# Second mixing stage: the squares of the last sixteen channels are added up by TensorE

## What is computed

```python
h = layer_norm(x, ni_w, ni_b)
h = (h @ pi_w.T + pi_b) * jax.nn.sigmoid(h @ gi_w.T + gi_b)
h = h * mask[..., None]
a1, b1, a2, b2 = jnp.split(h.astype(jnp.float32), 4, axis=-1)
x1 = jnp.einsum('bikd,bjkd->bijd', a1, b1)
x2 = jnp.einsum('bkid,bkjd->bijd', a2, b2)
h = jnp.concatenate([x1, x2], axis=-1).astype(h.dtype)
h = layer_norm(h, no_w, no_b)
return (h @ po_w.T + po_b) * jax.nn.sigmoid(h @ go_w.T + go_b)
```

## Time and profile before

| | |
|---|---|
| three timed runs | 1553.26, 1548.57, 1548.98 us, median 1548.98 |
| profiled execution | 1551.37 us, of which the span is 1549.5 |
| busy over the span | PE 89%, DVE 78%, ACT 63%, POOL 39% |
| granted TensorE clock, mean | 0.958 of 2.4 GHz |

### The profile page before, as it was taken

The page is one execution under the profiler, slowest core; times in us unless marked ns, Lnnn a source line. Parts: engine busy times, 40 slices in busy tenths (PEclk is TensorE's granted clock), DMA queues, the critical chain, the costliest instruction groups (busy, mean ns, idle before and its releaser), DMA issues. The chain is left out here.

```text
span 1549.5 us, 26748 instructions
## 1 busy us (share of the span) xinstructions
PE 1380.6 (89%) x9158; PEld 765.4 (49%) x9163; DVE 1213.9 (78%) x2073; ACT 977.9 (63%) x1576; POOL 607.1 (39%) x389
## 2 busy tenths in 40 slices
PE   6778897888797997999989999898999979997897
PEld 5427432222585442344469998222244447773443
DVE  6644787799699886999957776998799968998664
ACT  5675588834344787878846666356877856662555
POOL 6400298320000893299400000596359800003665
PEclk9898999999899998999989999899999999998999
DMA  9368210057785220499988886795189899996998
GB/s 356 130 190 313 96 55 2 1 164 205 264 296 206 83 94 1 164 336 341 345 304 299 306 299 226 272 373 215 46 331 344 341 325 391 418 395 230 392 389 313
DMA packets 152693, 381.62 MB, mean 246 GB/s; under 512 B 15728, under 2 KB 15984, under 8 KB 152432
## 3 DMA queue, kind: packets, MB, share of 16 engines
q1 hardware_dynamic: 140176, 356.64, 63.4%
q10 hardware_dynamic: 12384, 23.28, 4.1%
HBM read 191.11 MB, written 188.74 MB: 245 GB/s over the span
## 5 line engine op out<-in xcount | busy, mean ns | idle before, releaser
L1201 PE MATMUL banks<-work 128*128 128x256 f32 x1408 | 337.0, 388 | 16.1 <-DVE work L1274 6.7
L1201 PEld LDWEIGHTS banks<-work 128*128 128x128 f32 x1408 | 263.1, 196 | 63.3 <-issue 17.4
L1561 POOL TENSOR_TENSOR xT<-xT,work 128x512 f32<-128x512 f32 x192 | 241.3, 1273 | 58.9 <-DVE work L1610 56.0
L740 PE MATMUL banks<-work,w 64*64 64x512 f32 x2048 | 256.9, 595 | 3.3 <-DVE work L938 3.1
L978 DVE SCALAR_TENSOR_TENSOR work<-banks,bias,work 128x512 f32<-128x512 f32 x256 | 188.1, 748 | 29.7 <-PE banks L740 25.6
L856 ACT ACTIVATE work<-banks,bias 128x512 f32<-128x512 f32 x256 | 171.9, 686 | 42.1 <-PE banks L740 41.5
L1233 ACT COPY work<-banks 128x512 f32<-128x512 f32 x176 | 103.3, 587 | 144.9 <-PE banks L1201 141.0
L1372 POOL MEMSET work<- 32x2048 bf16 x4 | 7.2, 1800 | 469.2 <-issue 370.2
L1300 DVE TENSOR_TENSOR work<-work 128x512 f32<-128x512 f32 x176 | 121.2, 689 | 58.2 <-ACT work L1233 57.1
L1610 DVE SCALAR_TENSOR_TENSOR work<-banks,bias,work 128x512 f32<-128x512 f32 x192 | 142.0, 748 | 30.9 <-ACT work L1535 15.1
L909 POOL TENSOR_TENSOR work<-work,cols 128x512 f32<-128x512 f32 x2 | 163.9, 81970 | 0.3
(11 more groups left out here) (172 smaller groups left out, 2278.2 us busy)
## 6 DMA issues: line engine op xcount, KB each, us to landing
hidden_rows<-work SPq DMA_DIRECT2D x128, 512.0 KB, 4.1
work<-hidden_rows SPq DMA_DIRECT2D x120, 512.0 KB, 6.8
products<-work SPq DMA_DIRECT2D x88, 512.0 KB, 3.8
work<-products SPq DMA_DIRECT2D x88, 512.0 KB, 4.7
work<-gate_rows SPq DMA_DIRECT2D x64, 512.0 KB, 5.4
work<-hidden SPq DMA_DIRECT2D x40, 512.0 KB, 6.1
work<-in_x SPq DMA_DIRECT2D x32, 512.0 KB, 5.1
gate_rows<-work SPq DMA_DIRECT2D x32, 512.0 KB, 3.1
```

The lines of the kernel that those rows point to most:

```text
L740: mm = pe.matmul(out[side, :], w(name)[rows, side], h[rows, t % H, :], start=True, stop=True)
L1201: mm = pe.matmul(ZB[c % 2][:, r * N:r * N + N], a[:, kk, rows_of(r, c)], x[:, kk, :], start=(kk == 0), stop=(kk == 1))
L1561: pool.tensor_tensor(columns(t), columns(t), term[:, t % RING, :], ALU.add).then_inc(x_sb, 1)
```

## The change

For channels 16 to 31 of the second mixing stage, VectorE no longer adds the squares to `s2`. TensorE does, with products of the identity and the buffer of squares that accumulate in bank 7. The first of them (for channel 16) is preceded by one that brings in `s2` as it stands after 16 channels. `square_sums(c - 2)` follows `product(c - 1)` in the loop. The last one stands behind the clock-keeping products, which go to bank 6 now. ScalarE's square waits for the identity product of two channels back where it waited for VectorE. The variance step reads bank 7 in place of `s2`.

```diff
+    squares_on_tensor = masked_load
...
+            def square_sums(c):
+                if c < 0 or not squares_on_tensor(c):
+                    return
+                if c == turned:
+                    pe.wait_ge(s2_sb, turned)
+                    pe.matmul(bank[7][:, :], core.ident[:, :], s2, start=True, stop=False).then_inc(s2_mm, 1)
+                pe.wait_ge(sq_sb, c + 1)
+                pe.matmul(bank[7][:, :], core.ident[:, :], sq[:, c % 2, :], start=False,
+                          stop=c == channels - 1).then_inc(s2_mm, 1)
...
                 turn(c)
                 if c:
                     product(c - 1)
+                square_sums(c - 2)
             product(channels - 1)
-            core.keep_clock(pe, 4, bank[7])
+            square_sums(channels - 2)
+            core.keep_clock(pe, 4, bank[6])
+            square_sums(channels - 1)
...
-                at_least(act, s2_sb, c - 1)
+                if c >= 2 and squares_on_tensor(c - 2):
+                    act.wait_ge(s2_mm, c - turned)
+                else:
+                    at_least(act, s2_sb, c - 1)
...
                 dve.tensor_tensor(s1, s1, zs[:, c % (2 * OUT), :], ALU.add).then_inc(s1_sb, 1)
+                if squares_on_tensor(c):
+                    return
                 dve.wait_ge(sq_sb, c + 1)
...
-        finish(core, 1, 2, None, mask, sums, out)
+        finish(core, 1, 2, None, mask, [sums[0], core.bank[7]], out)
```

More of the change, by code:

```diff
@@ L1098, in mix @@
         (mask_in, mask_mm, mask_sb, masked_a, masked_b, turn_mm, ta_sb, tb_sb, z_mm, z_sb, sq_sb, s1_sb, s2_sb, begun,
-         shifted) = core.sems(f"mix{layer}", "mask_in mask_mm mask_sb masked_a masked_b turn_mm ta_sb tb_sb z_mm z_sb "
-                              "sq_sb s1_sb s2_sb begun shifted")
+         shifted, s2_mm) = core.sems(f"mix{layer}", "mask_in mask_mm mask_sb masked_a masked_b turn_mm ta_sb tb_sb z_mm "
+                                     "z_sb sq_sb s1_sb s2_sb begun shifted s2_mm")
         single = core.sems(f"mix{layer}", " ".join(f"single{c}" for c in range(SINGLES)))
@@ L1409, in on_tensor @@
     def on_tensor(self, pe):
-        self.core.keep_clock(pe, 4, self.core.bank[7])
+        self.core.keep_clock(pe, 4, self.core.bank[6])
         pe.wait_ge(self.rooted, 1)
-        self.core.keep_clock(pe, 4, self.core.bank[7])
+        self.core.keep_clock(pe, 4, self.core.bank[6])
     def first_factors(self, pe, nq, outs):
```

## The result

| | before | changed |
|---|---|---|
| timed runs with the prediction | median 1548.78 us (1547.15 to 1553.26, 4 runs) | median 1562.37 us (1558.49 to 1564.05, 4 runs) |
| ratio | | 1.0069, 95% interval 1.0046 to 1.0092 |
| the same kernels again (e1 below) | median 1550.74 us (30 runs) | median 1558.94 us (11 runs) |
| ratio | | 1.0048, 95% interval 1.0030 to 1.0065 |
| profiled execution | 1551.37 us | 1563.44 us |

The change makes the kernel slower. Forecast were 1556.2 us, a ratio of 1.0046, with a range from 1552 to 1560. The median of the first measurement lies 2.4 us above that range; its ratio, put on the 1548.98 us that the forecast stands on, gives 1559.7, just inside. The second, with more runs, lies inside by both. The ratios on record are not the quotients of the two medians, which are 1.0088 and 1.0053. A 31st run of the kernel before, at 7571.44 us, is not counted.

The account below looks back on a forecast made before the run. VectorE was taken to bound the stage at 2.41 us per channel, TensorE after the change at 2.59. A 7.1 us stage delay plus 0.06 for the variance step made 7.2; on the 1548.98 median, 1556.2 us, range 1552 to 1560.

Parts of the forecast that it names:

- The price of an identity product: On TensorE in the second mixing stage, each of seventeen identity products costs 0.86 us, taken from the first layer's gate products.
- The new pace: In the stage's last channels TensorE becomes the bound at 1.73 + 0.86 = 2.59 us per channel, against VectorE's 2.41 before.
- rival 1: Identity products share TensorE's array with neighbours, so not slower: 1548.4 us, or about 1541 at no price; chance 0.04.
- rival 2: Identity products run dearer on TensorE between products with other weights: 1558.8 us at 1.01 us each, 1561.7 at 1.18; chance 0.08.
- The lead of the first stretch: TensorE's lead from the first stretch is filled; with the slower pace, channel 31's copy starts at 493.5, 6.4 us later.
- The tail: Behind the last product, two identity products and four clock-keeping products take 3.45 us; barrier 3.7 us after the last copy's start.
- The variance step out of the bank: Reading the squares from a bank instead of SBUF makes this pass 0.750 us against 0.686, 0.06 us once.
- Waits that were to stay covered: In the second mixing stage, waits for squares, stores and the next stage's first loads stay hidden, at no cost.
- What the removal brings: VectorE loses sixteen passes of 0.60 us, leaving 1.81 us per channel and ending its masks at about 478.
- the free case: With identity products costing TensorE nothing, VectorE ends its masks at 478 and the stage 8 us early, so about 1541.
- The total: The whole kernel gets 7.2 us slower, to 1556.2 us on the median, 0.46%; chance 0.78.
- Rival 3: A busier stage end moves or removes TensorE's clock fall just behind the stage, a gain of 2.8 us: 1553.4; chance 0.10.

Follow-up runs that it names:

- e1: The changed kernel measured again with no edit, against the kernel before: ratio 1.0048, 44.21 us from the copy of channel 15 to the barrier.
- e4: The changed kernel with identity products over 256 of 512 columns for the sixteen channels: ratio 1.0006 to the kernel before, copies 2.16 us apart.
- e5: The changed kernel with VectorE also adding the sixteen squares, into a spare buffer: ratio 1.0048 to the kernel before, copies 2.59 us apart.
- e7: The changed kernel without the four clock-keeping products ahead of the last identity product: 43.16 us from copy 15 to barrier, one run of 1560.49 us.
- e6: The kernel before without VectorE's last sixteen passes over the squares and nothing in their place: ratio 0.9962, 33.72 us from copy 15 to barrier.
- e2: The kernel before with 23 instead of 4 clock-keeping products ending the second mixing stage, a pure delay: ratio 1.0051, 44.29 us from copy 15 to barrier.

## Why the prediction was right, and where it was not

- **The price of an identity product**, 0.86 us from the gate products of another stage: right. 476.33 to 477.19 in the timeline; e4 halves it with the columns.
- **The new pace**, 2.59 us per channel with TensorE as the bound: right to 0.01 us (e1, e5). With it falls rival 1 (room in the array) and rival 2 (a dearer product): all 32 records of L1213 last 592 or 593 ns.
- **The lead of the first stretch**: right. From the copy of channel 15 to that of channel 31 are 492.04 - 451.54 = 40.50 us; the steps forecast 493.5 - 452.92 = 40.6.
- **The tail**: right. From the last copy's start to the barrier 3.71 us against 3.7; e7 shows that 1.05 us of it hang on the clock-keeping products.
- **The variance step out of the bank**, 0.06 us: wrong, and without weight. L1402 takes 0.69 us, as long as it took from SBUF. The rows that it was taken from differ in more than the bank (see the last section).
- **Waits that were to stay covered** (squares, stores, loads of the next stage): right. In the changed kernel no copy waits for a store.
- **What the removal brings**: the prediction put the free case at 8 us early, about 1541. e6 has 3.4 us in the stage. The step that failed is "VectorE would end its masks at 478 and the stage some 3 us later": it left out that the transfers, which in the kernel before are full from 458 to 476 us (0.92 to 1.04 in each 2 us), would not follow a pace of 1.8 us. The means of the earlier trace rows, 0.78 and 0.74, do not show that. It carried no part of the forecast, only rival 1's far end.
- **The total**: 7.2 us forecast, 7.07 us in the stage, a ratio of 1.0048 in e1 and 1.0051 for the same delay without the change in e2. The first measurement's 1.0069 lies 3.6 us above the forecast. Its range up to 1560 gave the run-to-run spread too little room: single runs of one kernel spread over 10 us and more, and that the first ratio falls within it is partly luck. Rival 3, the clock behind the stage, did not come: there the lower level lies as before (0.59 from 506 to 512 us, against 0.54 in the earlier trace rows). What differs between the two executions lies in two other passages, and e1, e2 and e6 leave no need for a cost of the change there. That it was chance in the first four runs is the reading left over, not shown by itself.

## What to carry to other kernels

Work moved to an engine that idles a quarter of the time is free only up to that idle time per step: here 0.68 us were free and the product took 0.86, and the lead that the engine had built up was lost as well. What one engine is freed of pays only if the instructions queued behind it can start: four additions in a row gave nothing, the same number spread out gave 1.7 us. The four in a row also stood at the start, where TensorE had no time free in the kernel before; whether four in a row further back would do better was not tried. Where a total moves by other than the stage does, a pure delay of the same length shows whether the rest belongs to the change.

## What was not expected of the hardware

The times of the kernel before spread from 1546.85 to 1562.53 us in the 29 runs beside the last experiments. In two profiles, passages that do the same work differ by 2.6 and 4.0 us. In the second of them TensorE's clock lay longer at 1.2 GHz, in the first it did not. A pass of VectorE that read one operand from a bank took 0.69 us (L1402), while those of the earlier trace rows took 0.750; the latter take a bias column besides. The bank alone does not make the difference: L1287 and L1587 of the kernel before read a bank without such a column, at 0.686 us on average, like the passes from SBUF. What the column alone costs was not tried.
